# Scaling the results of a mixture-of-experts pass in groups of three blocks instead of two

## The reference

```python
x = x + layernorm(attention(layernorm(x)))          # recurrence over time, then Wo
h = layernorm(x)                                    # 16384 tokens x 256
probs = softmax(h @ router_w)                       # 8 experts
topw, topi = top_k(probs, 2)                        # each token goes to two of them
routed = sum over the two: topw * (silu(h @ w1[e]) @ w2[e])
shared = sigmoid(h @ shared_gate_w) * (silu(gate) * up @ shared_down)
x = x + layernorm(routed + shared)
```

## Time and profile before

| | |
|---|---|
| time, median of 3 runs | 1613.29 us (1612.08 to 1614.66) |
| profiled execution, its own time | 1613.5 us |
| its span, from the first to the last instruction | 1611.7 us |
| busy share: PE, PEld | 94%, 85% |
| busy share: DVE, ACT, POOL | 85%, 83%, 67% |
| granted TensorE clock, mean | 0.974 |
| second half of the expert part | from about 1346 us on |

### The profile page before, as it was taken

How to read it: one execution, slowest core, us unless ns; L and a number is a source line. 1 busy time by engine, 2 the same in 40 slices (tenths; PEclk the granted TensorE clock), 3 DMA queues, 4 the chain that set the end, 5 groups by cost and what they waited for, 6 DMA issues and landing times.

```text
span 1611.7 us, 35130 instructions
## 1 busy us (share of the span) xinstructions
PE 1518.8 (94%) x9960; PEld 1363.9 (85%) x9960; DVE 1377.9 (85%) x3140; ACT 1335.3 (83%) x2768; POOL 1082.7 (67%) x1168
## 2 busy tenths in 40 slices
PE   4899999999999999999999999689999998999992
PEld 3778888888888888888888888578999998999992
DVE  4799999999999999999989988856877777999993
ACT  3688898889888998999899888756777777999993
POOL 1146767767776777677667766756666664888886
PEclk9899999999999999999999999879999999999996
DMA  3112533343322222222322222228778763777771
GB/s 112 53 47 78 169 107 125 116 153 121 109 88 87 85 78 92 87 82 80 104 76 88 81 81 69 68 79 284 237 241 249 238 217 123 233 232 228 234 236 55
DMA packets 124619, 214.41 MB, mean 133 GB/s; under 512 B 19975, under 2 KB 67338, under 8 KB 124432
## 3 DMA queue, kind: packets, MB, share of 16 engines
q1 hardware_dynamic: 92368, 126.13, 26.5%
q0 software_dynamic: 32064, 86.04, 14.5%
HBM read 116.37 MB, written 99.39 MB: 134 GB/s over the span
## 4 chain that ended last, share of the span: by engine, by line
PE 61%; POOL 16%; issue 11%; DVE 5%; ACT 2%; DMA 1%; POOLq 0%; DVEq 0%; ACTq 0%; SPq 0%
PE PS L1453 51%; POOL d_ys L589 8%; POOL out L607 6%; PE PS L1445 3%; PE PS L1517 2%; PE PS L1515 2%; PE PS L1671 2%; POOL rsw L601 1%; PE PS L1687 1%; POOL d_xd L548 1%; DMA out<-vv,wqh 0%; POOL varw L599 0%; DVE st L1060 0%; PE PS L1652 0%; PE PS L1537 0%
## 5 line engine op out<-in xcount | busy, mean ns | idle before, releaser
L548 POOL DMA_INDIRECT d_xd<-h2n,ixs x248 | 312.0, 1258 | 193.8 <-DVE h2n L1178 127.6
L1453 PE MATMUL PS<-hTh,wqh 128*128 128x512 f32 x768 | 307.1, 400 | 16.0 <-ACT kk L644 10.8
L1453 PE MATMUL PS<-hTl,wqh 128*128 128x512 f32 x768 | 306.7, 399 | 0.0
L1453 PE MATMUL PS<-hTh,wql 128*128 128x512 f32 x768 | 306.2, 399 | 0.0
L1453 PEld LDWEIGHTS PS<-hTh,wqh 128*128 128x128 f32 x768 | 146.7, 191 | 50.9 <-ACT kk L644 11.7
L1453 PEld LDWEIGHTS PS<-hTh,wql 128*128 128x128 f32 x768 | 146.6, 191 | 34.5
L1453 PEld LDWEIGHTS PS<-hTl,wqh 128*128 128x128 f32 x768 | 146.8, 191 | 33.4
L555 POOL DMA_INDIRECT d_xs<-ysh,ixs x124 | 131.2, 1058 | 45.7 <-issue 45.4
L1687 PE MATMUL PS<-weh,h2h 128*128 x380 | 106.3, 280 | 0.0
L1687 PE MATMUL PS<-weh,h2l 128*128 x380 | 106.3, 280 | 0.0
L1687 PE MATMUL PS<-wel,h2h 128*128 x380 | 106.1, 279 | 0.0
(11 more groups left out here) (328 smaller groups left out, 5715.2 us busy)
## 6 DMA issues: line engine op xcount, KB each, us to landing
xin<-in_L_attn_x SPq DMA_DIRECT2D x32, 512.0 KB, 4.2
x<-in_L_attn_x SPq DMA_DIRECT2D x32, 512.0 KB
wqh<-d_xd SPq DMA_DIRECT2D x60, 272.0 KB, 3.6
wql<-d_xd SPq DMA_DIRECT2D x60, 272.0 KB, 3.4
d_xd<-zt SPq DMA_DIRECT2D x18, 272.0 KB
wel<-in_L_ffn_w SPq DMA_DIRECT2D x16, 256.0 KB, 5.1
d_xd<-h2n,ixs POOLq DMA_INDIRECT x248, 2.5
kk<-d_xs SPq DMA_DIRECT2D x12, 256.0 KB
```

What stands on the lines that cost most here:

```text
L548: g.indirect_dma_start(d_xd[s], bass.IndirectOffsetOnAxis(ap=ixs[:, m % 2, k:k + 1], axis=0), h2n_of(m)[:, j, :], None).then_inc(s_sct[s], 16)
L1453: ins = mm_(out_ap, l, r, start=(k == 0), stop=(k == len(todo) - 1))
```

## The change

Groups of three blocks take the place of pairs, with the last five blocks as one group of two and three of one (`SIZES`, `STARTS`; `group_of` gives a block's group and its place in it). POOL's list becomes: scale of group 0, and then block after block, with the scale of the next group placed ahead of the last block of each group. `final` comes one step of the loop later (`t-7`), and the loop is one step longer. The residual rows get six places: two more, in the room of `hf`. The buffers for the factors have six columns in each of the four groups instead of four, and the constant -0.5 has six. Every block's own arithmetic is the same.

```diff
-    NPAIR = (NB1 + 1) // 2
+    SIZES = [3] * ((NB1 - 5) // 3) + [2, 1, 1, 1]
+    STARTS = [sum(SIZES[:q]) for q in range(len(SIZES) + 1)]
+    NXK = 6
...
-        sqw = sb("sqw", [P, NPR, 4])
+        sqw = sb("sqw", [P, NPR, 6])
...
-        xk = [flat(t)[:, i * 2 * D:(i + 1) * 2 * D].rearrange("p (j d) -> p j d", j=2) for t in (ysh, xin) for i in range(2)]
+        xk = [flat(t)[:, i * 2 * D:(i + 1) * 2 * D].rearrange("p (j d) -> p j d", j=2) for t in (ysh, xin, hf) for i in range(2)]
...
+        def group_of(v):
+            q = max(g for g in range(len(SIZES)) if STARTS[g] <= v)
+            return q, v - STARTS[q]
...
             def last_scale(q):
-                many = min(2, NB1 - 2 * q)
-                at = slice(0, 2 * many)
-                pool.wait_ge(s_sqw, 2 * (2 * q + many))
+                at = slice(0, 2 * SIZES[q])
+                pool.wait_ge(s_sqw, 2 * STARTS[q + 1])
                 if q >= NPR:
-                    pool.wait_ge(s_fin, 4 * (q - NPR + 1))
+                    pool.wait_ge(s_fin, 2 * STARTS[q - NPR + 1])
...
-            for q in range(NPAIR + 1):
-                if q < NPAIR:
-                    last_scale(q)
-                for v in (2 * q - 2, 2 * q - 1):
-                    if 0 <= v < NB1:
-                        tokens_out(v)
+            last_scale(0)
+            for v in range(NB1):
+                if v + 1 < NB1 and group_of(v + 1)[1] == 0:
+                    last_scale(group_of(v + 1)[0])
+                tokens_out(v)
...
             def back_second(v):
-                if v >= 4:
-                    act.wait_ge(s_fin, 2 * (v - 3))
+                if v >= NXK:
+                    act.wait_ge(s_fin, 2 * (v - NXK + 1))
...
-            for t in range(NB + 6):
+            for t in range(NB + 7):
...
-                if t - 6 >= NB1:
-                    final(t - 6 - NB1)
+                if t - 7 >= NB1:
+                    final(t - 7 - NB1)
```

More of the change, by code:

```diff
@@ L53, in rwkv_moe @@
     NPR = 4
-    NPAIR = (NB1 + 1) // 2
+    SIZES = [3] * ((NB1 - 5) // 3) + [2, 1, 1, 1]
+    STARTS = [sum(SIZES[:q]) for q in range(len(SIZES) + 1)]
+    NXK = 6
+    assert STARTS[-1] == NB1
     NJ = N // BLK
@@ L148, in rwkv_moe @@
         ext = sb("ext", [P, 2, NT, NEXT])
-        sqw = sb("sqw", [P, NPR, 4])
-        varw = sb("varw", [P, NPR, 4])
-        rsw = sb("rsw", [P, NPR, 4])
-        mh4 = sb("mh4", [P, 4])
+        sqw = sb("sqw", [P, NPR, 6])
+        varw = sb("varw", [P, NPR, 6])
+        rsw = sb("rsw", [P, NPR, 6])
+        mh6 = sb("mh6", [P, 6])
         cnt = sb("cnt", [P, 2, E])
@@ L339, in rwkv_moe @@
         assert len(xb) == NX and len(yb) == NYB
-        xk = [flat(t)[:, i * 2 * D:(i + 1) * 2 * D].rearrange("p (j d) -> p j d", j=2) for t in (ysh, xin) for i in range(2)]
+        xk = [flat(t)[:, i * 2 * D:(i + 1) * 2 * D].rearrange("p (j d) -> p j d", j=2) for t in (ysh, xin, hf) for i in range(2)]
+        assert len(xk) == NXK
         xTh = [hTh[:, 0, 0:TC], rkh[:, 0, :]]
@@ L475, in _ @@
             g.memset(zero[:, :], 0.0).then_inc(s_const, 1)
-            g.memset(mh4[:, :], -0.5).then_inc(s_const, 1)
+            g.memset(mh6[:, :], -0.5).then_inc(s_const, 1)
             g.memset(ext[:, :, :, :], 0.0).then_inc(s_const, 1)
@@ L592, in last_scale @@
             def last_scale(q):
-                many = min(2, NB1 - 2 * q)
-                at = slice(0, 2 * many)
-                pool.wait_ge(s_sqw, 2 * (2 * q + many))
+                at = slice(0, 2 * SIZES[q])
+                pool.wait_ge(s_sqw, 2 * STARTS[q + 1])
                 if q >= NPR:
-                    pool.wait_ge(s_fin, 4 * (q - NPR + 1))
+                    pool.wait_ge(s_fin, 2 * STARTS[q - NPR + 1])
                 g.tensor_scalar(varw[:, q % NPR, at], sqw[:, q % NPR, at], 1.0 / D, EPS, ALU.mult, ALU.add).then_inc(s_vaw, 1)
                 pool.wait_ge(s_vaw, q + 1)
-                g.tensor_tensor(rsw[:, q % NPR, at], varw[:, q % NPR, at], mh4[:, at], ALU.pow).then_inc(s_rsw, 1)
+                g.tensor_tensor(rsw[:, q % NPR, at], varw[:, q % NPR, at], mh6[:, at], ALU.pow).then_inc(s_rsw, 1)
             def tokens_out(v):
@@ L900, in last_squares @@
             def last_squares(v):
-                w, q, k = NB1 + v, v // 2, v % 2
+                w = NB1 + v
+                q, k = group_of(v)
                 if q >= NPR:
@@ L913, in back_second @@
                 act.wait_ge(s_xb[w % NX], 16 * (w // NX + 1))
-                if v >= 4:
-                    act.wait_ge(s_fin, 2 * (v - 3))
-                A.activation(xk[v % 4][:, 1, :], xb[w % NX][:, 1, 0:D], ACT.Identity, bias=xb[w % NX][:, 1, C_EXT + 1:C_EXT + 2],
+                if v >= NXK:
+                    act.wait_ge(s_fin, 2 * (v - NXK + 1))
+                A.activation(xk[v % NXK][:, 1, :], xb[w % NX][:, 1, 0:D], ACT.Identity, bias=xb[w % NX][:, 1, C_EXT + 1:C_EXT + 2],
                              scale=xb[w % NX][:, 1, C_EXT:C_EXT + 1]).then_inc(s_backa, 1)
@@ L1389, in back @@
                 w = NB1 + v
-                if v >= 4:
-                    dve.wait_ge(s_fin, 2 * (v - 3))
-                V.tensor_scalar(xk[v % 4][:, 0, :], xb[w % NX][:, 0, 0:D], xb[w % NX][:, 0, C_EXT:C_EXT + 1], xb[w % NX][:, 0, C_EXT + 1:C_EXT + 2],
+                if v >= NXK:
+                    dve.wait_ge(s_fin, 2 * (v - NXK + 1))
+                V.tensor_scalar(xk[v % NXK][:, 0, :], xb[w % NX][:, 0, 0:D], xb[w % NX][:, 0, C_EXT:C_EXT + 1], xb[w % NX][:, 0, C_EXT + 1:C_EXT + 2],
                                 ALU.mult, ALU.add).then_inc(s_back, 1)
             def final(v):
-                w, q, k = NB1 + v, v // 2, v % 2
+                w = NB1 + v
+                q, k = group_of(v)
                 dve.wait_ge(s_rsw, q + 1)
@@ L1402, in final @@
                     V.scalar_tensor_tensor(out=t, in0=t, scalar=rsw[:, q % NPR, 2 * k + j:2 * k + j + 1],
-                                           in1=xk[v % 4][:, j, :], op0=ALU.mult, op1=ALU.add).then_inc(s_fin, 1)
-            for t in range(NB + 6):
+                                           in1=xk[v % NXK][:, j, :], op0=ALU.mult, op1=ALU.add).then_inc(s_fin, 1)
+            for t in range(NB + 7):
                 if t == 9:
```

## The result

The changed kernel takes 1638.94 us (median of 4 runs, 1635.98 to 1644.34) against 1613.79 (1612.08 to 1614.66): ratio 1.0162, 95% interval 1.0137 to 1.0187. It is slower, as forecast, but by 25 us and not by 6: outside the range, and beyond the price of the rival *POOL overfull* as well. The profiled execution took 1635.98.

The account below looks back on a forecast made before the run. VectorE was taken as the pace, POOL as a follower with just enough room, the twelve buffers as a close second limit. Terms 0 + 0 + 3.5 + 2.5 = +6.0 gave 1619.3 us, range 1611.5 to 1624.5.

Parts of the forecast that it names:

- POOL overfull: Rival, chance 0.11: VectorE's casts hold up POOL's transfers, 10.8 of 10.3 us a group; 10 us over the half, 1625.8 us.
- What POOL then does: POOL's second-pass transfers: backlog up to 4.8 us exceeds 3.44, so POOL catches up and waits for `final` itself.
- The loop: Twelve buffers, from `final` to reload: third blocks need 11.4 us against 10.7, so loads come late; +3.5 us, between 0 and 14.
- 1.2 us of cover: At VectorE's next `final`: it comes at 6.0, the power's result it needs at 4.8, so it would not wait.
- Fewer scales: POOL's scale instructions: 7 us less work over 66 blocks, worth 0 because VectorE keeps the pace.
- always in third blocks: Sign: TensorE's transposes wait for loads some five times or more, always at the third block of a group.
- The signs named beforehand: Expected in the changed profile: POOL idle until `final` ends, late loads in third blocks, four scales in the last 25 us.
- Single blocks at the end: POOL's last blocks: two more scales of one block at 1.26 us each; +2.5 us, bounds 0 and 2.5.
- Six places: Residual tiles: at most five are alive, so nobody waits; together with the wider memset, 0.

Follow-up runs that it names:

- the run without both suspects: Changed kernel with 15 buffers, second half: VectorE's SBUF cast replaced by a PSUM copy, subtraction's first input taken from PSUM; 1618.75 us, ratio 1.0039.

## Why the prediction was wrong

*The step that failed is "What POOL then does"*, and the price of "The loop" that rests on it. I let POOL catch up and wait for `final`, with transfers every 1.45 to 1.5 us, durations read in the phase of the kernel before. Out of that phase the six transfers take 1.24 us each in the mean, up to 1.63, and a group takes POOL 11.57 us for VectorE's 10.32. So POOL catches up only at the start of the half and behind late loads (13 waits for `final` in all) and falls back each time, and the "1.2 us of cover" of VectorE for the power's result turn into a wait of up to 1.5. The order of events in that step was right, as the run without both suspects shows (2.1, 2.1, 3.1); the lengths in it were not. That the kernel came out slower, as forecast, was luck: the +3.5 and +2.5 are not what made it so.

*"Fewer scales", 0.* Right for the kernel before only in that its VectorE row is full. But "nothing to spare" was read from an engine that stood in step with another one. That both were full in step, and the earlier trace rows, should have been the warning: 6.88 on POOL equalled twice 3.44 because POOL ran in step with VectorE's holds, not because it had room; 0.27 us more on it already cost 5 us. In the changed kernel with 15 buffers 1.44 us of scale less a group gave 35 us back.

*"The loop", +3.5 us.* Seen (13 waits for loads in 160 us), though not "always in third blocks": in the whole half 11 of the 21 blocks with under 0.25 us to spare are third ones. And yet it is not the price: with no load late the kernel is 12 us slower still. With pairs the term may well be right (5.5 us of waits). The signs named beforehand, POOL's waits for `final` and late loads, both appeared and did not tell this account from the rival that was right.

*"Single blocks at the end", +2.5.* The end is 5.2 us longer, but at most 1.2 of that through them, and without singles the time is no lower. The four small scales stand in the trace, from 1605.05 to 1619.38.

*"Six places" and the memset, 0.* No row shows a wait for a place; not tested alone.

*The rival "POOL overfull", 0.11.* The mechanism was this one; its price was 10 us for the half and should have been 22. Its sum was 9.5 us of own work plus 3 x 0.42 for the casts = 10.8. The runs give the terms as differences: own work 9.5 to 9.8, casts 12.07 - 10.77 = 1.3, and 10.77 less the own work, 1.0 to 1.3, that I did not have, for the three subtractions with two SBUF inputs, 0.3 to 0.4 each. What `final` and `back` hold is still in the own work. The 12.07 are those of 15 buffers; with twelve, late loads bring it to 11.57. I gave it a low chance since "the rows bear out a tenth or two per transfer, no more": those rows came from the one phase in which that is so. The Trainium skill, "SBUF — State Buffer", section "SBUF: two separate sides", which I cited for it, names VectorE instructions with two SBUF inputs as well as the copies, against instructions of GpSimd that read SBUF, and says that whichever side starts first keeps the shared port for its whole instruction. The runs agree on the inputs, with 1.0 to 1.3 us a group and the 0.06 behind `final`, and on holds in both directions, with the 0.13 of `back`. They do not bear out a hold for the whole of a transfer: without the suspects 38 of 59 `back`s lie wholly inside a transfer and take 0.39 to 0.41 us.

What stays open: what makes the gap of about 1 us that broke the phase with 15 buffers; why groups of three do not fall into a phase as good as that of the kernel before (pairs with a later `final` do, up to the gap); what `back`, which also goes from SBUF to SBUF, costs POOL; and how the 9 us of the pairs divide. One of the 16 runs of the kernel before in the first comparison took 1627.62 us, where a lost phase would put it; it left no trace. That the phase is lost is shown by POOL's and VectorE's rows, not by an experiment that puts it back; in the trace of the pairs with twelve buffers it comes back by itself, behind late loads: POOL's lag, up to 6.4 us at block 48, is 2.8 and 2.1 from block 56 to 62, and blocks 63 to 69 take 3.44 us.

## What to carry to other kernels

Two engines that are both full and in step, with waits that name only "issue", may be holding each other: then the durations of the one are those of this phase alone, and no term of a sum may be taken from them for another order. Look for the longest and the shortest instance of the same instruction elsewhere in the trace (here 0.97, 1.20, and 1.27 in the first half) and price the change with both. When an engine's list is lengthened in what it must do between two events, test it first by taking work out of that list; one run told more than any count of waits.

## What was not expected of the hardware

VectorE's cast from SBUF to SBUF (0.42 us) lengthens POOL's work by about its whole length when POOL runs against it (0.43 each) and by nothing that shows in the phase of the kernel before. A POOL transfer of 128 rows spans 0.97 to 1.96 us in these traces, and the spread shrinks where the cast and the subtraction are taken away (0.98 to 1.27). More buffers made three kernels slower, by 9 to 16 us (a fourth by 6, which is not clear of noise), though their loads landed 9.6 us or more early in the mean. In the groups of three a late load is also a pause in which POOL catches up; in the other two the loss begins with the gap of 1 us.
